# Cross attention's residual in a decoder layer: beta added on GpSimd, the LayerNorm finished on VectorE, loops written out

## The reference, cut to what matters

```python
x = _layernorm(x + self_attention(x))          # x1 below
x = _layernorm(x + cross_attention(x, ctx))    # x2 below
x = _layernorm(x + feed_forward(x))

# inside cross_attention, behind its output projection:
delta = rs * (ctx @ Wo.T + bo)                 # y is the bracket; rs is a clipped scalar
mu  = delta.mean(axis=-1, keepdims=True)
var = jnp.mean((delta - mu) ** 2, axis=-1, keepdims=True)
delta = (delta - mu) / jnp.sqrt(var + EPS_LN) * ln_gamma + ln_beta
```

## Time and profile before

| what | value |
|---|---|
| median of 3 runs | 1569.08 us (1567.79 to 3576.67) |
| the profiled execution | 1567.61 us, span 1565.8 us |
| issue of the DMA of beta (L923) on SP | 1003.6 us |
| cross attention, from the first scores (1020.4) to the last x2 (1368.5) | 348.1 us |
| busy over the whole span | PE 91%, DVE 81%, ACT 53%, POOL 45% |
| bodies 2 to 5 (1096.1 to 1262.2), of 166.1 us | PE 143.5, DVE 148.9, ACT 94.6, POOL 108.0 us busy |

### The profile page before, as it was taken

How to read it: one execution, slowest core, us unless ns; L and a number is a source line. 1 busy time by engine, 2 the same in 40 slices (tenths; PEclk the granted TensorE clock), 3 DMA queues, 4 the chain that set the end, 5 groups by cost and what they waited for, 6 DMA issues and landing times.

```text
span 1565.8 us, 25940 instructions
## 1 busy us (share of the span) xinstructions
PE 1426.8 (91%) x8658; PEld 1132.0 (72%) x8658; DVE 1267.0 (81%) x2109; ACT 826.7 (53%) x1950; POOL 710.5 (45%) x765
## 2 busy tenths in 40 slices
PE   5999999999999999999999999789888897289997
PEld 4788888888888888888888887667666674134454
DVE  6988888888888888888878887357899988778885
ACT  4444444544544444545555564465555565068875
POOL 4434334334334335335235232644666666446554
PEclk9999999999999999999999999899999998589999
DMA  5401201201101100011121112300000004000000
GB/s 203 162 9 33 68 1 41 67 1 41 56 12 41 53 15 28 26 63 48 41 89 47 41 48 68 108 28 13 10 8 14 13 1 168 0 1 21 28 27 35
DMA packets 31399, 69.48 MB, mean 44 GB/s; under 512 B 4022, under 2 KB 4534, under 8 KB 30908
## 3 DMA queue, kind: packets, MB, share of 16 engines
q1 hardware_dynamic: 31292, 68.24, 12.9%
HBM read 59.83 MB, written 8.40 MB: 44 GB/s over the span
## 4 chain that ended last, share of the span: by engine, by line
PE 50%; DVE 29%; issue 10%; POOL 6%; ACT 2%; DVEq 1%; DMA 1%; SPq 0%; POOLq 0%; ACTq 0%
PE psum L326 9%; PE psum L327 8%; PE psum L328 8%; DVE rope_b L513 6%; PE psum L1546 3%; PE psum L1518 3%; PE psum L367 3%; DVE p L522 3%; DVE total_e L526 3%; DVE acc L556 2%; DVE s L494 2%; PE psum L1535 2%; PE psum L388 2%; DVE rope_a L513 2%; PE psum L934 2%
## 5 line engine op out<-in xcount | busy, mean ns | idle before, releaser
L730 POOL TENSOR_TENSOR qk<-rope_a,rope_b 128x512 f32<-128x512 f32 x128 | 177.2, 1384 | 568.8 <-DVE rope_b L513 568.8
L326 PE MATMUL psum<-x_hi,w_hi 128*128 128x512 f32 x512 | 210.1, 410 | 11.2 <-POOL w_lo L724 11.2
L328 PE MATMUL psum<-x_hi,w_lo 128*128 128x512 f32 x512 | 201.4, 393 | 0.0
L327 PE MATMUL psum<-x_lo,w_hi 128*128 128x512 f32 x512 | 200.6, 392 | 0.0
L513 DVE SCALAR_TENSOR_TENSOR rope_b<-psum,qk_bias,sin 64x512 f32<-64x512 f32 x256 | 192.0, 750 | 3.7
L604 ACT ACTIVATE e<-s 128x384 f32<-128x384 f32 x128 | 66.3, 518 | 243.0 <-DVE s L494 243.0
L1277 ACT ACTIVATE xe<-xe,mask_now 128x256 f32<-128x256 f32 x256 | 132.4, 591 | 105.8 <-DVE xe L1079 105.8
L494 DVE SCALAR_TENSOR_TENSOR s<-psum,tri 128x384 f32<-128x384 f32 x128 | 70.7, 552 | 121.3 <-PE psum L367 121.3
L326 PE MATMUL psum<-w_hi,x_hi 128*128 128x256 f32 x512 | 147.4, 288 | 0.0
L327 PE MATMUL psum<-w_lo,x_hi 128*128 128x256 f32 x512 | 144.7, 283 | 0.0
L328 PE MATMUL psum<-w_hi,x_lo 128*128 128x256 f32 x512 | 144.6, 282 | 0.0
(11 more groups left out here) (183 smaller groups left out, 3962.1 us busy)
## 6 DMA issues: line engine op xcount, KB each, us to landing
stage<-w_self_dram SPq DMA_DIRECT2D x64, 256.0 KB, 2.9
w_raw<-w_ffn_dram SPq DMA_DIRECT2D x32, 512.0 KB, 3.6
acc<-xT_dram SPq DMA_DIRECT2D x4, 1024.0 KB, 7.6
acc<-x_dram SPq DMA_DIRECT2D x1, 4096.0 KB, 15.0
w_signs<-w_sign SPq DMA_DIRECT2D x16, 256.0 KB, 2.1
c_raw<-ctxT_dram SPq DMA_DIRECT2D x8, 512.0 KB, 3.5
xstage<-w_cross_dram SPq DMA_DIRECT2D x16, 256.0 KB, 2.9
w<-w_signs SPq DMA_DIRECT2D x2, 2048.0 KB, 11.8
```

Source lines behind the costliest of these rows:

```text
L326: pe.matmul(ps, ah, bh, start=n == 0, stop=False)
L327: pe.matmul(ps, ah, bl, start=False, stop=False)
L328: last = pe.matmul(ps, al, bh, start=False, stop=n == len(pairs) - 1)
L730: nc.gpsimd.tensor_tensor(qk[:, k % 2, which, :], rope_a[:, which, :], rope_b[:, which, :], ALU.add).then_inc(qk_ready, 1)
```

## The change

1. POOL's `keep_x` now writes acc = x1 + beta (two 128x512 instructions, chunk 2, ahead of the root of y and of `add_bias`). ACT's copies go.
2. DVE finishes y of sequence b-1 in chunk 3 of the next body instead of b-2 a body later: (y - mean) * gamma, twice, then times rstd plus acc, twice; all four are SCALAR_TENSOR_TENSOR with two SBUF tensors each. `scale_y`, POOL's six instructions and `finish_last` go.
3. `sum_statistics` of b-1 follows at once in chunk 3. POOL's root of it and DVE's `x2_norm` and `x2_max` now come in chunk 0 of the body after.
4. `take_y` no longer waits for `summed`; bodies 2 to 5 are written out.

```diff
-            for b in (-1, 0, 1):
-                emit(b, b % 2)
-            with eng.Fori(0, (B - 4) // 2) as i:
-                for j in range(2):
-                    emit(i * 2 + (2 + j), j)
-            for b in range(B - 2, B + 2):
+            for b in range(-1, B + 2):
                 emit(b, b % 2)
...
             def take_y(b, par, j):
                 dve.wait_ge(o_mm, b * 2 + j + 1)
-                wait(dve, summed, b * 2)
...
-            def scale_y(b, par):
+            def finish_y(b):
                 dve.wait_ge(rooted[1], b + 1)
-                wait(dve, z_done, b * 2)
                 nc.vector.tensor_scalar(rstd_s[:], rstd[:, 1, :], rs[:], None, ALU.mult).then_inc(scaled, 1)
+                if isinstance(b, int) and b == 0:
+                    dve.wait_ge(affine_in, 32)
+                for j in range(2):
+                    nc.vector.scalar_tensor_tensor(y[:, j, :], y[:, j, :], mv[:, 1, j, 0:1], gamma[:],
+                                                   ALU.subtract, ALU.mult).then_inc(z_done, 1)
                 dve.wait_ge(scaled, b + 1)
                 for j in range(2):
-                    nc.vector.tensor_scalar(y[:, j, :], y[:, j, :], mv[:, 1, j, 0:1], rstd_s[:, j:j + 1],
-                                            ALU.subtract, ALU.mult).then_inc(z_done, 1)
+                    tile = acc[:, tile_at(b, j), :]
+                    dve.wait_ge(z_done, b * 2 + j + 1)
+                    dve.wait_ge(x1_kept, b * 2 + j + 1)
+                    nc.vector.scalar_tensor_tensor(tile, y[:, j, :], rstd_s[:, j:j + 1], tile, ALU.mult, ALU.add
+                                                   ).then_inc(summed, 1)
...
                     if i == 0:
                         if live(b, 2):
-                            scale_y(b - 2, par)
+                            x2_norm(b - 2)
+                            x2_max(b - 2)
...
-                    if i == 3 and live(b, 2):
-                        x2_norm(b - 2)
-                        x2_max(b - 2)
+                    if i == 3 and live(b, 1):
+                        finish_y(b - 1)
+                        sum_statistics(b - 1)
...
-            def finish_y(b, par):
-
-                for j in range(1 if isinstance(b, int) and b == B - 1 else 2):
-                    tile = y[:, j, :]
-                    pool.wait_ge(z_done, b * 2 + j + 1)
...
+            def keep_x(b):
+                if isinstance(b, int) and b == 0:
+                    pool.wait_ge(affine_in, 32)
+                for j in range(2):
+                    pool.wait_ge(x1_ready, b * 2 + j + 1)
+                    nc.gpsimd.tensor_tensor(acc[:, tile_at(b, j), :], x1[:, j, :], beta[:], ALU.add
+                                            ).then_inc(x1_kept, 1)
...
-                    if i == 3 and live(b, 2):
-                        root(2, b - 2, (x2_ready, (b - 2) * 2))
...
                     if i == 0 and live(b, 2):
-                        finish_y(b - 2, par)
+                        root(2, b - 2, (x2_ready, (b - 2) * 2))
...
                     if i == 2:
+                        if live(b + 1):
+                            keep_x(b + 1)
+                        if live(b, 1):
+                            root(1, b - 1, (scaled, b - 1))
```

More of the change, by code:

```diff
@@ L876, in cross_attention @@
         z_done = sem("z_done")
-        gammaed = sem("gammaed")
-        betaed = sem("betaed")
         summed = sem("summed")
-        last_step = sem("last_step")
         env["shared_sems"].update(kq_mm=kq_mm, kq_out=kq_out, x1_kept=x1_kept, c_ready=c_ready, xw_ready=w_ready,
@@ L1263, in round_x @@
                                ).then_inc(t_rounded, 1)
-            def keep_x(b, j):
-                act.wait_ge(x1_ready, b * 2 + j + 1)
-                nc.scalar.copy(acc[:, tile_at(b, j), :], x1[:, j, :]).then_inc(x1_kept, 1)
             def exps(b, par, c, heads):
@@ L1307, in emit @@
                             take_q(nb, npar, 0)
-                            keep_x(nb, 0)
-                            keep_x(nb, 1)
                         else:
@@ L1397, in emit @@
                                 add_bias(b + 2)
-                        if live(b, 1):
-                            root(1, b - 1, (scaled, b - 1))
             bodies(pool, emit)
```

## The result

The changed kernel takes **1594.9 us** (median of 4 runs, 1593.95 to 1596.41) against 1568.43 before: ratio 1.0169, 95% interval 1.0155 to 1.0183. That is 26.5 us slower, where 1600 and a range of 1562 to 1614 had been given. One of the four runs of the kernel before took 3576.67 us, which nothing on record explains; the other three lie between 1567.38 and 1569.08. The changed kernel's profiled execution has a span of 1593.0 us, 27.2 more than before.

A forecast was written before the change was run, and what follows sets the result against it. With PE and DVE both near full, the order of waits was taken to decide. Stall and collisions in the bodies, less 9.8 at the tail, summed to +30.8 on 1567.6; with 1.5 for the median, 1600 us, range 1562 to 1614.

The forecast's parts named there:

- The new stall: Chunk 0: DVE's x2_norm waits for its root, queued on POOL behind e_sum; 4.4 us a body.
- The collisions: Chunk 3: DVE's rstd_s and two-input passes take turns with POOL's instructions; 6.5 us a body, bounded by 0 and 6.5.
- the sign: Chunk 3: the four new passes taking 6 to 8 us together instead of 2.5 would show the forecast right.
- Clip 3: Middle body: chunk 3's clip, waiting for its scores, comes 32.2 us after the body's first clip.
- The sum, stretch by stretch: Whole kernel: gains and losses of the bodies, start and tail added up to +30.8 us.
- Before the first scores: Body -1: POOL's keep_x waits for beta and its first pass meets the last L1198, ahead of Q; +1.2 us.
- The two-input pass: DVE: a pass with two SBUF tensors costs 0.6 us to the next start when uncontended.
- Loops written out: Bodies 2 to 5: writing them out priced at 0, bounds -2 (register work) and +3 us (code fetch).
- Rival B: Chunk 3: collisions do not bite, each body 6.5 us shorter than forecast; 1563 us, 15%.
- D: Chunk 0: the new stall hides because PE, not DVE, sets the body; 1552 us, 7%.
- Rival C: PE's clock: one more block at 1.2 GHz, 1.5 to 2.9 us more in six bodies; 1608 to 1616 us, 15%.

The follow-up runs named there:

- e2: Changed kernel with POOL's root for x2 moved ahead of chunk 0's e_sum: 1581.97 us, ratio 1.0087 to the kernel before.
- e5: e4 with one exchange on DVE in chunk 0, the previous body's division ahead of rstd_s and the four two-input passes: 1557.68 us, ratio 0.9933.
- e3: e2 plus POOL's bias and beta passes moved from chunk 2 to chunk 0: 1574.29 us, ratio 1.0039.
- e4: Changed kernel, same arithmetic, DVE's two-port instructions put where POOL is idle, POOL's bias, beta and x2 root moved: 1544.17 us, ratio 0.9851.
- e1: Kernel before with bodies 2 to 5 written out and nothing else changed: 1566.37 us against 1568.25, ratio 0.9987.
- e8: Kernel before, loops written out, only the last two sequences finished the new way: 1558.16 us, ratio 0.9933.
- e7: e4 with the mask's copy moved from the end of chunk 3 to chunk 0 behind the division: 1544.39 us, ratio 0.9846.
- e6: Changed kernel with ACT copying x1 to acc as before and beta's addition left out: 1587.14 us, ratio 1.012.

## Why the prediction was right, and where it was off

- **The new stall** for x2's root was forecast at 4.4 us and is 4.40, by the queue's order that the earlier trace rows gave. Shown by e2: 12.9 us of the loss. I had 16: in chunk 3 more passes then meet c_lo and e_sum, so part of what the root's place wins is given back, and bodies 2 and 3 gained little at clip 2, which no run explains.
- **The collisions** were put at 6.5 us a body (mask 0.2, rstd_s 1.1, passes 5.2). Measured in body 4 against the same times without turns: mask 0.5, rstd_s 1.2, passes 2.9, together 4.6. The four passes took 5.3 us, where 6 to 8 had been named as the sign. The mechanism was right, the size too high by 1.9: clip 3 came late, rstd_s met c_lo instead of the bias, and one pass fewer had to wait. In body 1, with clip 3 on time, the passes take 7.4 us, 4.9 more than alone. Shown by e5 and by e3, and e4 is free of them for the passes.
- **Clip 3** was too early in my chain by 1.7 us (33.86 against 32.2): 1.5 of it since the Q block ran mostly at 1.2 GHz, which I had kept as a rival of its own. That the body still comes out at 47.56 against 47.95 is not two errors that happen to cancel. POOL's queue in chunk 3 counts from clip 2; it was forecast to end at 43.4 and ended at 43.95, and DVE's passes can only end behind it. A later clip 3 only meets less of it.
- **The sum, stretch by stretch** (forecast, then measured): body 1 +7.2, +6.6; bodies 2 to 5 +25.7, +23.4; body 6 +5.9, +6.4; body 7 +0.6, -0.8; end -9.8, -9.5. Body 0 took 36.2 instead of 36.9, which I had at 0.
- **Before the first scores** I had +1.2 and measured +1.6 (1022.03 against 1020.40), a right number for a wrong reason. POOL's beta pass did wait for beta's DMA and met L1198, but the four L1198 took 2.49 us as before, and DVE's take-over of the values ahead of them, before the beta pass began (1010.18), was 2.8 us late already (1008.24 against 1005.43). e1, which has no such pass, has its first clip at 1022.29. What shifts this stretch stays open.
- **The two-input pass** costs 0.66 us between starts alone, 0.6 was taken from the earlier trace rows.
- **Loops written out**: priced 0 from two bodies of equal length, measured -1.9 in e1. No run shows the 0.5 us of register work in the lower bound. Held against e1's bodies 2 to 5 (162.8 us), the stall and the collisions cost 26.7 us there, not 23.4.
- **Rival B** (collisions do not bite) and **D** (the stall hides) fall by e5 and e2. **Rival C** (the clock): the clock did fall, from 0.98 to 0.91 over the middle bodies, and five Q blocks ran low. It was not tried apart, but body 1 beside bodies 2 to 5 of the same trace puts its price at 0.2 us a body, some 1 us of the 26.5, not the 1.5 to 2.9 a body that I had; DVE waited for PE nowhere else for more than 0.4 us in the middle bodies.
- What the description of the change says is true: POOL has less to do and the statistics come sooner. Where the change put its work, it cost 27 us. With the work placed, e4 is 24 us faster than the kernel before, but that is not all the arithmetic's: 1.9 are the loops (e1), 8.2 the end (e8), and about 14 are left for the bodies. Nor was the kernel before given the same care with places, though its own pair of L1152 takes 3.06 us on e_sum; how much of the 14 that would bring no run tells.

## What to carry to other kernels

When work is moved from GpSimd to VectorE, list which VectorE instructions read two SBUF tensors, and which scale or copy from SBUF to SBUF (the L1152 pair, 3.06 us on e_sum instead of 1.00; the mask's 128x4 copy, 1.14 to 1.61 in e4 instead of 0.16 alone), and set them against GpSimd's timeline: behind a clip from PSUM with GpSimd idle the five took 2.8 us, on top of e_sum 6.4. A short instruction on an in-order queue that another engine waits for belongs ahead of the long one that waits for something late: one root of 0.7 us was worth 13 us. A replay of one body by its rows, engine by engine, gave +30.8 us for a measured +27.2. Its inner steps were off by up to 1.9 us; the end of the body held, since it hung on the one queue that was forecast well.

## What the runs showed that was not expected

- VectorE's passes slow GpSimd too: two bias passes 3.45 us instead of 2.54, the low part 1.18 to 1.20 instead of 0.73.
- Written-out bodies were faster than the hardware loop here by 1.9 us in all (ratio 0.9977 to 0.9996), though 0.79 MB of instructions were fetched instead of 0.72.
- Moving the mask's copy from one e_sum to another (e7) gave nothing: 1544.39 against 1544.17 us.
- What a late clip 3 costs depends on POOL's queue. In the change one that came 1.5 us later cost a body 0.2 us; in e6, where the queue is shorter, one that came 1.1 us later cost 1.7 (from clip 2 to the end 21.4 us in bodies 3 and 4, 23.1 in bodies 2 and 5).
